# Cross-attention and quantised feed-forward on one core: score maxima copied from one head's block, output normalisation behind head 9, high-part output products first and six of them ahead of the maxima's transposes

## The chip, the core and the metric

The kernel runs on 1 core of one Trainium2 chip. The metric is device time in microseconds (us); smaller is better. Engines are called PE (matrix products), DVE (vector), ACT (activations, copies), POOL (GpSimd) and SP (it issues all DMAs).

## The reference, cut to what matters

There are 16 batches of 256 tokens with 512 features. For every batch:

```python
q = rope(layernorm(x) @ wq.T); k = rope(ctx @ wk.T); v = ctx @ wv.T      # 16 heads of 32
scores = q @ k.T * sqrt(32)          # only |position difference| <= 128 counts
attn = softmax(scores)               # scores are large: the row maximum has to be taken off
x = x + (attn @ v) @ wo.T + wo_b
x = x + ffn(layernorm(x))            # gelu between two matmuls whose inputs are rounded to 16 bit integers
```

The feed-forward part needs the largest absolute value of all normalised rows of all batches before it can begin, and the largest of the hidden layer before its second matmul.

## The kernel before, in words

**Stages.** Stage A (up to some 765 us) does attention batch by batch. Stage B (to some 1,012 us) does the first feed-forward matmul and GELU over 8 tiles of 512 tokens, stage C the second. The change touches stage A alone.

**One step of stage A.** Step b (`step` in each engine's program; `steps` calls it for b = 0 to 15) does three batches at once: the scores, softmax and weighted values of batch b; the projections of batch b+1 (absent in step 15); the output projection of batch b-1 (absent in step 0). So steps 1 to 14 have everything. Every float32 product that needs precision is made of three passes over values split into a high and a low part.

PE's order in a step is written out by hand. First come the 16 heads' scores (`scores`, L597), head pair by head pair, with the projection work of batch b+1 as filling: after pair 0 and 1 the k tiles (and, with pair 1, the transposes of x, L526), after pair 2 the first half of v, after pairs 3 and 4 the q tiles (L514 to L516), after pairs 5 and 6 six products each of the second half of v. The scores go to a ring of two banks, so head n waits until the maximum of head n-2 has been read out (L595). Behind head 15, `o_products` of batch b-1 begins: 24 products (L581), 12 for each half (128 tokens) of the batch, handed out by `some(count)`. Some come before `max_transposes` (L609), four behind it, the rest between the 16 transposed score products (`scores_t`, L631). After heads 7, 11 and 15 of these, and at the end, a `clump` multiplies probabilities with values (L645) and sums the denominators (L658).

DVE's order in a step: masked row maxima of heads 0 to 15 (`row_maxima`, L1063, two passes of 128 rows a head, each followed by a read-out of the maximum), with other work behind the head pairs: behind pair 0 `invert` (L1104, the reciprocal of the denominators of batch b-1, which also frees the bank for PE's x transposes), behind pair 1 `xt_rest`, behind pairs 2 and 3 `rotate` of k (L1086, L1087, L1089), behind pair 5 (head 11) the two `normalise` operations (L1110), which multiply the outputs of batch b-1 by the inverted denominators. Behind head 15 come `split_max` (L1068, L1070: negated maxima in a high and a low part), `rotate` of q, the residual additions, layer norm moments, the quantisation of one weight block and layer norm 1 of batch b+2. 

ACT: after `normalise`, `ot_lead` (L841) rounds the outputs to their high part `t_hi`; after `max_transposes`, two `max_copy` operations (L857) write the maxima as rows 96 to 127 of `q_st` for heads 0 and 1, then for heads 2 and 3; then the 16 exponentials (L864). POOL: `bias_x` (L1374), the low parts of k (`split_lo`, L1358, four operations), the low parts `t_lo` of the outputs (`ot_rest`, L1369), then one band selection a head (L1381).

**The denominators' way.** `invert` writes them to `neg_max`; SP's `spread_shares` stores them to DRAM (L349), waits, and loads them back spread over the rows that need them (L352) into `probs`, called shares here. `normalise` waits for that load. SP issues in program order; in front of these two DMAs stands the load of x_res (L318), which waits until the previous store of it has landed. At the head of step 15, SP first issues two loads of stage B (L357).

**The maxima's way.** `stack_max` (L341 to L344): when both `max_copy` operations are done, SP copies the 32 rows of heads 0 to 3 to heads 4 to 7, 8 to 11 and 12 to 15, three DMAs of 128 KB within SBUF. The transposed scores of heads 4, 8 and 12 wait for one each. All heads have the same rows: each row block of 256 values is repeated for every head.

```python
pe.wait_ge(ot_hi, 2 * j + s + 1)      # L570, in o_products, before its 12 products
pe.wait_ge(ot_lo, 2 * j + s + 1)      # L571
some(4); max_transposes(b, has_proj); some(4)
for n, count in enumerate((1, 2, 2, 3, 1, 1, 1, 0, 1, 1, 1, 0, 1, 1, 0, 0)):
    scores_t(b, n, has_o, has_proj); some(count)
```

Of the kernel before, what the change touches and what calls it, by code (L numbers as in the profile page):

```python
# [22 lines left out]
F32 = mybir.dt.float32  # L23
# [6 lines left out]
P = 128  # L30
NB, S, D = 16, 256, 512
# [3 lines left out]
KC = D // P  # L35
# [3 lines left out]
MROW = 3 * DK  # L39
# [44 lines left out]
def build(nc, t):  # L84
# [12 lines left out]
    with ExitStack() as ctx:  # L97
        def sem(name):
            return ctx.enter_context(nc.semaphore(name))

        def sb(name, shape, dt=F32, where=ctx):
            return where.enter_context(nc.sbuf_tensor(name, shape, dt))
# [16 lines left out]
        w_hi, w_lo = {}, {}  # L119
# [7 lines left out]
        q_st = sb("q_st", [P, H, S], F32R, pa)  # L127
# [5 lines left out]
        t_hi = sb("t_hi", [P, KC, S], F32R, pa)  # L133
        t_lo = sb("t_lo", [P, KC, S], F32R, pa)
# [55 lines left out]
        kv_bank = bank[2:4]  # L190
# [14 lines left out]
        ot_hi, ot_lo = sem("ot_hi"), sem("ot_lo")  # L205
        c_hi, c_lo = sem("c_hi"), sem("c_lo")
        v_mm, o_mm, v_done = sem("v_mm"), sem("o_mm"), sem("v_done")
# [5 lines left out]
        max_stacked = [sem(f"max_stacked{i}") for i in range(1, NC4)]  # L213
        s_mm, max_done, msplit, mT_mm, mT_done = (sem(n) for n in ("s_mm", "max_done", "msplit", "mT_mm", "mT_done"))
# [29 lines left out]
        MAX_COPIES = 2  # L244
# [60 lines left out]
        def _(sp):  # L305
# [32 lines left out]

            def stack_max(b):

                sp.wait_ge(mT_done, MAX_COPIES * (b + 1))  # L341
                for i in range(1, NC4):
                    sp.dma_start(q_st[MROW:P, KC * i:KC * (i + 1)].bitcast(F32),
                                 q_st[MROW:P, 0:KC].bitcast(F32)).then_inc(max_stacked[i - 1], 16)  # L344

            def spread_shares(j):

# [145 lines left out]
            for i in range(NT):  # L493
                for f in range(FC):
                    n, g = (i - KEPT, f + LOADS) if f + LOADS < FC else (i - KEPT + 1, f + LOADS - FC)
# [14 lines left out]
        def _(pe):  # L510
# [7 lines left out]
            def x_transposes(j, s):  # L518

                if s == 0:  # L520
                    pe.wait_ge(ln1_norm, 2 * j + 2)
                    wait(pe, wt_done, j - 1)
                    wait(pe, den_done, j - 1)
                    wait(pe, rope_step["q"], ROPE_OPS * j)
                for c in range(KC):
                    mm = pe.transpose(q_bank[s][:, c * P:(c + 1) * P], x_ln[:, s, c * P:(c + 1) * P], ident[:])  # L526
                mm.then_inc(xt_mm, 1)
# [38 lines left out]
            def o_products(j, has_proj):  # L566

                for s in range(2):
                    tok = slice(s * P, (s + 1) * P)
                    pe.wait_ge(ot_hi, 2 * j + s + 1)  # L570
                    pe.wait_ge(ot_lo, 2 * j + s + 1)  # L571
                    if s == 0:
                        pe.wait_ge(w_lo_done, 5)
                    if has_proj:
                        pe.wait_ge(rope_step["k"], ROPE_OPS * (j + 3))
                    else:
                        pe.wait_ge(res_done, 2 * j)
                    for c in range(KC):
                        parts = ((t_hi, "hi"), (t_hi, "lo"), (t_lo, "hi"))
                        for m, (part, w) in enumerate(parts):  # L580
                            mm = pe.matmul(kv_bank[s][:], part[:, c, tok], (w_hi if w == "hi" else w_lo)["wo"][:, c],  # L581
                                           start=c == 0 and m == 0, stop=c == KC - 1 and m == 2)
                            if c == KC - 1 and m == 2:
                                mm.then_inc(o_mm, 1)
                            yield

            def scores(b, n):

                if n % KC == 0:
                    for name in ("k", "q"):  # L590
                        pe.wait_ge(stacked[name][n // KC], STAGED * (b + 1))
                if n < 2:
                    wait(pe, exp_done, H * b)
                else:
                    pe.wait_ge(max_done, 2 * (H * b + n - 1))  # L595
                for qb in range(2):
                    mm = pe.matmul(ring[n % 2][:, qb * S:(qb + 1) * S], q_st[0:MROW, n, qb * P:(qb + 1) * P],  # L597
                                   k_st[0:MROW, n], start=True, stop=True)
                mm.then_inc(s_mm, 1)

            def max_transposes(b, has_proj):

                pe.wait_ge(msplit, 2 * (b + 1))
                if has_proj:
                    pe.wait_ge(v_done, 2 * (b + 2))
                else:
                    pe.wait_ge(oT_out, 2 * b)
                for qb in range(2):
                    mm = pe.transpose(pv_bank[1][:, qb * P:(qb + 1) * P], neg_max[:, qb], ident[:])  # L609
                mm.then_inc(mT_mm, 1)  # L610
# [89 lines left out]
            def step(b, par, has_c, has_o, has_proj, has_xt):  # L700

                tiles = [[] for _ in range(H // 2)]
                if has_proj:
                    tiles[0] += [lambda: qk_tile(b + 1, "k", 0)]
                    tiles[1] += [lambda: x_transposes(b + 1, 0), lambda: x_transposes(b + 1, 1), lambda: qk_tile(b + 1, "k", 1)]
                    tiles[2] += [lambda: v_tile(b + 1, 0)]
                    tiles[3] += [lambda: qk_tile(b + 1, "q", 0)]
                    tiles[4] += [lambda: qk_tile(b + 1, "q", 1)]
                    tiles[5] += [lambda: v_tile(b + 1, 1, range(2))]
                    tiles[6] += [lambda: v_tile(b + 1, 1, range(2, KC))]  # L710
                for n in range(H):
                    scores(b, n)
                    if n % 2:
                        for tile in tiles[n // 2]:
                            tile()


                heavy = o_products(b - 1, has_proj) if has_o else iter(())

                def some(count):  # L720
                    for _ in range(count):
                        next(heavy, None)

                some(4)
                max_transposes(b, has_proj)
                some(4)
                for n, count in enumerate((1, 2, 2, 3, 1, 1, 1, 0, 1, 1, 1, 0, 1, 1, 0, 0)):
                    scores_t(b, n, has_o, has_proj)
                    some(count)
                    if n in (7, 11, 15):  # L730
                        clump(b, par, n // KC - 1, has_proj)
                assert next(heavy, "none") == "none"
                w_transposes(b, has_proj)
                clump(b, par, NC4 - 1, has_proj)
# [286 lines left out]
        def _(dve):  # L1021
# [77 lines left out]
            def xt_rest(j, s):  # L1099
                rest(q_bank, s, xt_hi, 2 * j + s + 1, xt_lo)  # L1100
# [5 lines left out]
            def normalise(b, half):  # L1106
                dve.wait_ge(oT_out, 2 * b + half + 1)
                dve.wait_ge(share_in, 16 * (b + 1))
                part = oT[:, 2 * half:2 * half + 2].rearrange("p i t -> p (i t)")
                dve.tensor_tensor(part, part, share[:, 2 * half * S:2 * (half + 1) * S], ALU.mult).then_inc(onorm, 1)  # L1110
# [62 lines left out]
            def step(b, par, has_c, has_o, has_proj, has_xt):  # L1173

                between = {p: [] for p in range(H // 2)}
                if has_o:
                    between[0] += [lambda: invert(b - 1)]
                    between[5] += [lambda: normalise(b - 1, 0), lambda: normalise(b - 1, 1)]
                if has_proj:
                    between[1] += [lambda: xt_rest(b + 1, 0), lambda: xt_rest(b + 1, 1)]  # L1180
                    between[2] += [lambda: rotate(b + 1, "k", 0)]
                    between[3] += [lambda: rotate(b + 1, "k", 1)]
                for n in range(H):
                    row_maxima(b, n)
                    if n % 2:
                        for work in between[n // 2]:
                            work()
                split_max(b)
                if has_proj:
                    rotate(b + 1, "q", 0)  # L1190
                    rotate(b + 1, "q", 1)
                if has_o:
                    residual(b - 1, 0)
                    ln2_moments(b - 1, 0)
                quantise_win(b)
                if has_xt:
                    ln1(b + 2)
                if has_o:
                    residual(b - 1, 1)
                    ln2_moments(b - 1, 1)  # L1200
                    largest(b - 1, 0)
                    largest(b - 1, 1)
# [253 lines left out]
```

## Time and profile before

| what | value |
|---|---|
| runs | median 1253.18 us of 3 (1250.85 to 1253.63) |
| the profiled execution, its own time | 1251.07 us |
| its span, first to last instruction | 1249.3 us |
| mean granted PE clock | 0.970 of full |
| PE busy | 1138.1 us, 91% of the span |
| DVE busy | 981.0 us, 79% |
| ACT / POOL busy | 639.6 / 366.4 us |
| one full step of stage A | 43.5 to 44.9 us; granted clock 1.00 from 110 us to 678 us |

Start times are in us from the start of the span. Busy times include overlap of pipelined operations. A matmul's row gives its duration including the pipeline; the distance between two starts says what it costs in a stream. "x4" is a row that merges four instructions; a bracket tells how long the engine was idle before it and who ended the wait.

### The profile page before, as it was taken

The numbers are of one execution on the slowest core, as the hardware profiler recorded it, in microseconds if no ns is written. First come the engines' busy times: TensorE is split into PE (matmuls) and PEld (weight loads), VectorE is DVE, ScalarE is ACT, GpSimd is POOL, SyncE is SP. The second block draws the span as 40 slices with busy tenths as digits, with TensorE's granted clock in tenths as the row PEclk, the third lists the DMA queues.
The fourth block names the chain that finished last, engine by engine and source line by source line (L and its number), as shares of the span: only waits on it lengthen the run. The fifth ranks groups of instructions, "written<-read, shape, count | busy, mean of one in ns | idle before, by whom it ended". The sixth has DMA issues, their size and how long they took to land.

```text
span 1249.3 us, 23318 instructions
## 1 busy us (share of the span) xinstructions
PE 1138.1 (91%) x7776; PEld 759.7 (61%) x7776; DVE 981.0 (79%) x2527; ACT 639.6 (51%) x1000; POOL 366.4 (29%) x540
## 2 busy tenths in 40 slices
PE   5889999999999899999999665999999979999997
PEld 5767777787777688677768443444444434444443
DVE  6769989989988988988899545666666678888885
ACT  5254355335435534543553243555655458777774
POOL 1136336344533634453363220000000030112220
PEclk9889999999999999999999787999999989999999
DMA  8453575566456447545644711455554400567762
GB/s 270 110 143 106 158 178 137 139 183 155 108 161 177 131 134 194 140 120 164 177 119 114 218 56 69 160 206 198 208 188 143 152 0 35 186 224 249 219 207 92
DMA packets 96055, 191.44 MB, mean 153 GB/s; under 512 B 13392, under 2 KB 24912, under 8 KB 95952
## 3 DMA queue, kind: packets, MB, share of 16 engines
q1 hardware_dynamic: 95952, 190.14, 51.5%
q8 instruction: 56, 0.92, 0.3%
q14 instruction: 47, 0.39, 0.1%
HBM read 89.43 MB, written 44.04 MB: 107 GB/s over the span
## 4 chain that ended last, share of the span: by engine, by line
PE 38%; DVE 31%; issue 24%; DMA 3%; SPq 2%; ACT 2%; POOL 0%; DVEq 0%; ACTq 0%; POOLq 0%
PE bank L792 17%; DVE bank L1063 6%; PE bank L514 4%; PE bank L515 4%; PE bank L516 4%; DVE bn L1024 3%; PE bank L597 2%; DVE roped L1089 2%; DVE neg_max L1104 2%; DVE rt L1086 2%; DVE row_max L1063 2%; DVE rt L1087 2%; DVE x_res L1056 1%; PE bank L526 1%; PE bank L581 1%
## 5 line engine op out<-in xcount | busy, mean ns | idle before, releaser
L1063 DVE CUSTOM_DVE_ANT_0 bank<-bank,mask 128x256 f32<-128x256 f32 x512 | 201.4, 454 | 54.6 <-PE bank L597 48.0
L792 PE MATMUL bank<-wout_int,g_hi 128*128 128x512 bf16 x512 | 195.8, 382 | 8.8 <-DVE g_lo L1336 8.7
L792 PE MATMUL bank<-wout_int,g_lo 128*128 128x512 bf16 x512 | 195.6, 382 | 0.0
L761 PE MATMUL bank<-qT_hi,win_int 128*128 128x512 bf16 x512 | 194.2, 379 | 1.4 <-DVE qT_lo L1254 1.4
L761 PE MATMUL bank<-qT_lo,win_int 128*128 128x512 bf16 x512 | 194.1, 379 | 0.0
L864 ACT ACTIVATE probs<-bank 128x512 f32<-128x512 f32 x256 | 142.4, 603 | 52.8 <-PE bank L631 48.3
L1381 POOL TENSOR_SCALAR_AFFINE_SELECT probs<-probs 128x256 f32<-128x256 f32 x256 | 109.1, 430 | 82.9 <-ACT probs L864 78.6
L1336 DVE TENSOR_TENSOR g_lo<-h_int,g_hi 128x512 f16<-128x512 f32 x128 | 104.3, 815 | 35.6 <-ACT g_hi L991 34.3
L597 PE MATMUL bank<-k_st,q_st 96*128 96x256 f32 x512 | 98.4, 306 | 25.7 <-DVE row_max L1063 19.3
L1374 POOL TENSOR_TENSOR x_res<-x_res,wo_b 128x512 f32<-128x512 f32 x32 | 42.0, 1332 | 243.9 <-DMA x_res<-in_x 231.1
L964 ACT ACTIVATE h_ring<-bank,b_in,g_scale 128x512 f32<-128x512 f32 x96 | 73.5, 778 | 75.2 <-PE bank L761 58.1
L1278 DVE TENSOR_REDUCE hmax<-h_ring 128x512 f32 (+1 forms) x96 | 63.4, 682 | 60.6 <-ACT h_ring L964 58.6
L631 PEld LDWEIGHTS bank<-q_st,k_st 128*128 128x128 f32 x512 | 90.3, 193 | 31.8 <-issue 13.6
L597 PEld LDWEIGHTS bank<-k_st,q_st 96*128 96x128 f32 x512 | 76.8, 195 | 50.1 <-DVE row_max L1063 30.8
L631 PE MATMUL bank<-q_st,k_st 128*128 128x256 f32 x512 | 104.1, 294 | 3.1 <-DMA q_st<-q_st 2.0
L991 ACT CAST g_hi<-h_int 128x512 f16<-128x512 f32 x128 | 78.7, 615 | 39.6 <-PE bank L792 31.4
L792 PEld LDWEIGHTS bank<-wout_int,g_hi 128*128 128x128 f16 x512 | 50.4, 98 | 71.4 <-issue 11.2
L1421 POOL TENSOR_TENSOR xq<-xq,b_out 128x512 f32<-128x512 f32 x32 | 48.3, 1540 | 154.5 <-DMA xq<-x_scratch 147.7
L761 PEld LDWEIGHTS bank<-qT_hi,win_int 128*128 128x128 bf16 x512 | 50.1, 98 | 62.3 <-DVE qT_lo L1254 3.1
L792 PEld LDWEIGHTS bank<-wout_int,g_lo 128*128 128x128 f16 x512 | 50.4, 98 | 61.0 <-issue 1.6
L761 PEld LDWEIGHTS bank<-qT_lo,win_int 128*128 128x128 bf16 x512 | 50.1, 98 | 59.2
L514 PE MATMUL bank<-cT_hi,wk_hi 128*128 128x256 f32 x256 | 74.5, 291 | 12.6 <-DVE cT_lo L1141 12.6
(146 smaller groups left out, 2666.2 us busy)
## 6 DMA issues: line engine op xcount, KB each, us to landing
hidden_scratch<-h_ring SPq DMA_DIRECT2D x96, 256.0 KB, 2.0
h_ring<-hidden_scratch SPq DMA_DIRECT2D x96, 256.0 KB, 3.0
k_st<-k_hi SPq DMA_DIRECT2D x128, 128.0 KB, 2.5
q_st<-q_hi SPq DMA_DIRECT2D x128, 128.0 KB, 2.4
xq<-x_scratch SPq DMA_DIRECT2D x16, 1024.0 KB, 6.2
x_ln<-in_x SPq DMA_DIRECT2D x16, 512.0 KB, 4.5
ctx_raw<-in_ctxT SPq DMA_DIRECT2D x16, 512.0 KB, 4.9
k_st<-k_lo SPq DMA_DIRECT2D x64, 128.0 KB, 2.7
```

The costliest lines, as they stand in the source:

```text
L514: pe.matmul(out, l_hi, r_hi, start=first, stop=False)
L597: mm = pe.matmul(ring[n % 2][:, qb * S:(qb + 1) * S], q_st[0:MROW, n, qb * P:(qb + 1) * P], k_st[0:MROW, n], start=True, stop=True)
L631: mm = pe.matmul(third[n][:, kb * S:(kb + 1) * S], k_st[:, n, kb * P:(kb + 1) * P], q_st[:, n], start=True, stop=True)
L761: mm = pe.matmul(bank[f % 4][:], win_int[:, c, f * P:(f + 1) * P], part[:, par, c], start=c == 0 and part is qT_hi, stop=c == KC - 1 and p ...
L792: mm = pe.matmul(bank[4 * par + u][:], part[:, f % 4, u * P:(u + 1) * P], wout_int[:, f], start=f == 0 and part is g_hi, stop=f == FC - 1 ...
L864: act.activation(probs[:, n % SLOTS].rearrange("p k q -> p (k q)"), third[n][:], ACT.Exp, scale=SCORE_SCALE).then_inc(exp_done, 1)
L964: act.activation(dst, bank[f % 4][:], ACT.Gelu, bias=b_in[:, f:f + 1], scale=g_scale[:, f:f + 1]).then_inc(gelu_done, 1)
L991: act.copy(g_hi[:, f % 4], h_int[:, f % 4]).then_inc(ghi_done, 1)
L1063: dve.tensor_tensor_reduce(sc, sc, mask[:, (1 - qb) * P:(1 - qb) * P + S], 1.0, NEG, ALU.add, ALU.max, row_max[:, qb, n:n + 1]).then_inc(m ...
L1278: dve.tensor_reduce(hmax[:, bass.ds(FC * n + f, 1)], src, AX_X, ALU.max, apply_absolute_value=True).then_inc(hmax_done, 1)
L1336: dve.tensor_tensor(g_lo[:, f % 4], h_int[:, f % 4], g_hi[:, f % 4], ALU.subtract).then_inc(glo_done, 1)
L1381: pool.affine_select(out=far, in_=far, compare_op=ALU.is_ge, fill=0.0, base=1 - P, pattern=[[0, 2], [1, P]], channel_multiplier=1).then_in ...
```

## The change

The copy of the maxima now waits for the first `max_copy` only, and takes one head's block (head 0) as its source, repeated over the four heads of each destination. `normalise` goes from behind pair 5 (head 11) to behind pair 4 (head 9). In `o_products` the eight products of `t_hi` of each half come first and the wait for `t_lo` stands behind them, in front of the four products of `t_lo`. Six products instead of four come before `max_transposes`, and one fewer each behind the transposed scores of heads 3 and 13.

```diff
             def stack_max(b):
-                sp.wait_ge(mT_done, MAX_COPIES * (b + 1))
+                sp.wait_ge(mT_done, MAX_COPIES * b + 1)
                 for i in range(1, NC4):
                     sp.dma_start(q_st[MROW:P, KC * i:KC * (i + 1)].bitcast(F32),
-                                 q_st[MROW:P, 0:KC].bitcast(F32)).then_inc(max_stacked[i - 1], 16)
+                                 q_st[MROW:P, 0:1].bitcast(F32).to_broadcast([P - MROW, KC, S])).then_inc(max_stacked[i - 1], 16)
...
                     pe.wait_ge(ot_hi, 2 * j + s + 1)
-                    pe.wait_ge(ot_lo, 2 * j + s + 1)
...
                     for c in range(KC):
-                        parts = ((t_hi, "hi"), (t_hi, "lo"), (t_lo, "hi"))
-                        for m, (part, w) in enumerate(parts):
-                            mm = pe.matmul(kv_bank[s][:], part[:, c, tok], (w_hi if w == "hi" else w_lo)["wo"][:, c],
-                                           start=c == 0 and m == 0, stop=c == KC - 1 and m == 2)
-                            if c == KC - 1 and m == 2:
-                                mm.then_inc(o_mm, 1)
+                        for w in (w_hi, w_lo):
+                            pe.matmul(kv_bank[s][:], t_hi[:, c, tok], w["wo"][:, c], start=c == 0 and w is w_hi, stop=False)
                             yield
+                    pe.wait_ge(ot_lo, 2 * j + s + 1)
+                    for c in range(KC):
+                        mm = pe.matmul(kv_bank[s][:], t_lo[:, c, tok], w_hi["wo"][:, c], start=False, stop=c == KC - 1)
+                        if c == KC - 1:
+                            mm.then_inc(o_mm, 1)
+                        yield
...
-                some(4)
+                some(6)
                 max_transposes(b, has_proj)
                 some(4)
-                for n, count in enumerate((1, 2, 2, 3, 1, 1, 1, 0, 1, 1, 1, 0, 1, 1, 0, 0)):
+                for n, count in enumerate((1, 2, 2, 2, 1, 1, 1, 0, 1, 1, 1, 0, 1, 0, 0, 0)):
...
                 if has_o:
                     between[0] += [lambda: invert(b - 1)]
-                    between[5] += [lambda: normalise(b - 1, 0), lambda: normalise(b - 1, 1)]
+                    between[4] += [lambda: normalise(b - 1, 0), lambda: normalise(b - 1, 1)]
```

## Rows read from the trace of the kernel before

**Rows 1.** Chain of waits, 360 to 420 us: start, duration, engine, tile and line
```profile
373.17 0.68 DVE rt L1086
...
396.22 1.06 PE bank L526 x8
...
410.47 0.31 DVE bank L1063
```

**Rows 2.** Timeline of DVE, step 7, heads 9 to 15: start, duration, instruction, [idle before]
```profile
365.93 0.14 DVE L1063 DVE_READ_ACCUMULATOR2_ANT row_max<- 128x1 f32 x1
366.87 0.43 DVE L1063 CUSTOM_DVE_ANT_0 bank<-bank,mask 128x256 f32<-128x256 f32 x1 [0.80 <-PE bank L597]
...
368.36 1.29 DVE L1110 TENSOR_TENSOR oT<-oT,probs 128x512 f32<-128x512 f32 x2
...
371.94 0.43 DVE L1063 CUSTOM_DVE_ANT_0 bank<-bank,mask 128x256 f32<-128x256 f32 x1
```

**Rows 3.** Timeline of POOL, step 7, same stretch
```profile
365.37 2.83 POOL L1358 TENSOR_TENSOR k_lo<-roped,k_hi 128x256 fp32r<-128x256 f32 x4 [1.75 <-ACT k_hi L810]
```

**Rows 4.** Timeline of DVE, then of POOL, step 2
```profile
149.11 1.19 DVE L1110 TENSOR_TENSOR oT<-oT,probs 128x512 f32<-128x512 f32 x1
...
146.94 2.81 POOL L1358 TENSOR_TENSOR k_lo<-roped,k_hi 128x256 fp32r<-128x256 f32 x4 [1.71 <-ACT k_hi L810]
```

**Rows 5.** Timeline of DVE, then of POOL, stage C
```profile
1020.47 1.54 DVE L1336 TENSOR_TENSOR g_lo<-h_int,g_hi 128x512 f16<-128x512 f32 x1
1021.93 1.49 DVE L1315 TENSOR_SCALAR h_int<-h_int,wout_man 128x512 f32<-128x512 f32 x1
...
1021.43 1.70 POOL L1421 TENSOR_TENSOR xq<-xq,b_out 128x512 f32<-128x512 f32 x1
```

**Rows 6.** Timeline of PE, step 7, heads 13 to 15
```profile
370.06 0.40 PE L516 MATMUL bank<-wv_hi,cT_lo 128*128 128x512 f32 x1
370.49 0.50 PE L597 MATMUL bank<-k_st,q_st 96*128 96x256 f32 x2
...
373.31 0.44 PE L609 MATMUL bank<-ident,neg_max 128*128 128x128 f32 x2 [0.39 <-DVE neg_max L1070]
```

**Rows 7.** Timeline of DVE, first pass of head 10, steps 1 and 14
```profile
104.01 0.43 DVE L1063 CUSTOM_DVE_ANT_0 bank<-bank,mask 128x256 f32<-128x256 f32 x1 [0.65 <-PE bank L597]
...
673.88 0.43 DVE L1063 CUSTOM_DVE_ANT_0 bank<-bank,mask 128x256 f32<-128x256 f32 x1 [0.34 <-PE bank L597]
```

**Rows 8.** Line L352 (shares) summed up; its issue in step 11; DVE, head 9 there
```profile
DMA to landing us min/median/max: 3.5/3.7/5.3
...
537.08 0.58 SPq L352 DMA_DIRECT2D probs<-den_scratch  x1
...
541.76 0.14 DVE L1063 DVE_READ_ACCUMULATOR2_ANT row_max<- 128x1 f32 x1
```

**Rows 9.** Landing of L343 (maxima), of L349 (denominators); PE, head 4, step 8
```profile
DMA to landing us min/median/max: 2.2/2.3/4.0
...
DMA to landing us min/median/max: 1.7/3.9/7.2
...
422.59 0.50 PE L631 MATMUL bank<-q_st,k_st 128*128 128x256 f32 x2 [1.30 <-DMA q_st<-q_st]
```

**Rows 10.** Timelines of ACT (head 4), of DVE and of PE behind `split_max`, step 7
```profile
377.77 0.60 ACT L864 ACTIVATE probs<-bank 128x512 f32<-128x512 f32 x1 [0.34 <-PE bank L631]
...
386.19 0.68 DVE L286 SCALAR_TENSOR_TENSOR nt_t<-nt_t,veps 128x2 f32<-128x2 f32 x1
...
392.73 0.42 DVE L1063 CUSTOM_DVE_ANT_0 bank<-bank,mask 128x256 f32<-128x256 f32 x1
...
391.71 0.74 PE L597 MATMUL bank<-k_st,q_st 96*128 96x256 f32 x4
```

**Rows 11.** Timeline of DVE, then of PE, step 15 and the end of stage A
```profile
719.84 1.29 DVE L1110 TENSOR_TENSOR oT<-oT,probs 128x512 f32<-128x512 f32 x2 [7.71 <-DMA probs<-den_scratch]
...
753.42 0.76 PE L581 MATMUL bank<-wo_hi,t_hi 128*128 128x512 f32 x1 [10.29 <-ACT t_hi L841]
```

## The prediction, made before the changed kernel was run

> **What bounds the kernel now.** I read the chain of waits first, then the timelines of DVE, PE and POOL around the lines that the change moves. The busy shares (PE 91%, DVE 79%) are averages over three stages. In stage A the chain of waits changes engines three times in a step [rows 1]: from `split_max` (373.1) it lies on DVE without a gap, through rotation, moments, weight block and layer norm, up to `invert`; at 396.22 it goes to PE, whose x transposes need the bank that `invert` frees; at 410.47 it comes back to DVE at head 10 and stays there, through `normalise` and heads 12 to 15, until PE's transposes of the maxima. So DVE is the bound behind `split_max` and again behind head 10; PE is it between. The x transposes start 23.2 us behind `split_max` (373.06 in this step) in 11 of steps 1 to 13, 23.5 in step 6 and 24.4 in step 8.
>
> **Normalisation behind head 9.** First what it gives. In step 7 the last maximum of head 9 is read out from 365.93 and DVE idles until head 10's scores come, at 366.87 [rows 2]: 0.94 us, into which a part of `normalise` now fits. `normalise` costs 1.21 us (368.36 to the head 12 start at 369.57).
>
> Then what it meets. POOL's four low-part operations of k run from 365.37 to 368.20 [rows 3], 0.70 us each: head 9 ends 0.55 us into them, in every step. `normalise` now comes behind them. The trace shows what a DVE operation with two operands in SBUF does beside such an operation of POOL. In step 2 the first `normalise` took 1.19 us where 0.68 is the median: POOL ended 0.64 behind its start, and it ended 0.55 later [rows 4]. In stage C they take turns: DVE's operation from 1020.47 ends 0.58 behind POOL's (1021.43), POOL's next takes 1.70 where the one before took 1.26, and DVE's next, begun at 1021.93, ends behind that one [rows 5]. The Trainium skill says the same more sharply (SBUF — State Buffer, Who interferes with whom): a DVE instruction with two SBUF inputs and a GpSimd instruction that reads SBUF lock one another out for a whole instruction. By that rule moving `normalise` here is the wrong way round, and the trace agrees.
>
> The block worked out from head 9's read-out: 0.15 until POOL's current operation ends, 0.57 for the first `normalise`, 0.57 for POOL's next (0.73, less the overlap of their ends), 0.55 for the second, less 0.08 until the next maximum can begin: 1.76 us. Bounds: 1.21 if they don't meet, 2.5 if the second waits for two. I take 1.76: the rows are of the same kinds of instruction, and one of them is `normalise` beside this very operation.
>
> Step 7 then: head 10 begins at 365.93 + 1.76 = 367.69, not 366.87; head 11 0.73 later, 368.42; its maximum is out and seen by PE 0.96 later, 369.38. Head 13's scores wait for that (ring of two banks). Behind them come 0.33 and six v products at 0.235, so head 14's scores start at 371.12 instead of 370.49 [rows 6] (370.06 + 0.235 is where PE would have been by itself), DVE takes head 14 0.59 behind that and head 15 0.73 later: 372.44 instead of 371.94 [rows 2]. All of step 7 costs +0.50. In general, with i the time between head 9's read-out and head 10, and B the length of the present block, the cost is 1.44 - i - (B - 1.21). I read i and B in all 14 steps (head 10 of the first and last: [rows 7]): in seven i is 0.72 to 0.95 and B 1.21, cost 0.49 to 0.72, together 3.9; in the other seven i is 0.13 to 0.59 and B up to 1.72, cost 0.79 to 0.81, together 5.6. **Sum +9.5.**
>
> **Shares.** `normalise` waits for L352, which lands 3.5 to 5.3 us behind its issue [rows 8]. At head 9 it has landed in 11 steps. In three it has not: step 3 by 0.32, step 8 by 0.23, step 11 by 0.62 (537.08 + 5.3 against 541.76 [rows 8]); each then meets one more POOL operation, 0.70. **+2.1.** Behind the waiting `normalise` stand the maxima 10 and 11, and behind these PE's heads 12 and 13. SP, ACT and POOL queues keep their order; `t_lo` comes earlier, and PE needs it three products or more later: no cost.
>
> **Copy of the maxima.** SP issues it 0.53 us earlier, one `max_copy`. Head 4 now comes one product (0.235) earlier, so it needs the DMA to land within 2.45 + 0.53 - 0.24 = 2.74 us; it lands in 2.3 at the median [rows 9]. Its source rows are now runs of 1 KB instead of 4 KB. The nearest row with 1 KB runs and 128 KB is L349: 1.7, 3.9 and 7.2, but that goes to DRAM and mostly behind another DMA. I take 2.3 and keep 1.7 and 3.9. The Trainium skill (DMA: Bandwidth & Descriptors, Why small descriptors are slow) puts the penalty of small pieces on HBM alone; by it the landing stays and the sum too. In step 8 the copy landed late and PE waited 1.30 [rows 9]: 0.3 less of it.
>
> **Six products ahead.** Between head 15's scores and the transposes PE idles 0.39 behind four products [rows 6], and by my step 7 it would idle 0.7 behind six: two products (0.47) go into a hole, no cost. Head 4's transposed scores come one product earlier; ACT idled 0.34 there for PE [rows 10], so exponentials, POOL's band selections and low parts move up by 0.235. PE's own gain is worth nothing at first, since DVE is the bound there: it takes head 0 1.02 behind PE's start (392.73 against 391.71 [rows 10]) where 0.69 would do. But DVE's layer norm chain is paced by POOL: an operation on two values a row takes 0.68 beside it [rows 10]. I take 0.2 of the 0.235 for the 13 steps (1 to 13) that run on into `invert`; bounds 0 and 0.33. With step 8: **-2.9.** The product taken from behind head 13 gains nothing: the last clump waits for ACT and POOL. High part first: the same 24 products, no cost.
>
> **Step 15 and the end.** The shares are late there by 7.71 us [rows 11]. Heads 10 and 11 were done in that wait; now they stand behind it, two of 0.75, and PE's heads 12 and 13 behind them (products stand 0.43 apart there, not 0.235, after PE's long wait). Worked through as above, `split_max` comes 1.96 later than now; six products at that distance end at about the same time: **+1.9** (1.5 to 2.8). At the end the output products start with `t_hi` done (752.65) instead of behind `t_lo` (753.42 [rows 11]): **-0.7.**
>
> **Sum:** 9.5 + 2.1 - 2.9 + 1.9 - 0.7 = +9.9 us on the profiled execution's own 1251.07, so 1261. That execution lies 2.1 below the median of the runs; 9.9 on the median is 1263. I say 1262.
>
> **Rivals.** (a) *The two engines don't meet*, or POOL yields: the block is 1.21. Then 0.55 less in 14 steps and some 1.3 less for the late shares: +0.9, 1252 to 1255. For it: in seven present steps they don't meet; against: the overlap at the new place is there in all 14. (b) *Faster:* the maxima 10 and 11 don't hold PE, since PE's filling covers them; head 14 and 15 come as PE can bring them, head 15 at 371.62 instead of 371.94, 0.32 in 14 steps, and with -2.9, +1.9 and -0.7 it is -6.2: 1245 to 1247. It decides at head 10: its start must not be over 0.3 us later than now. For it: the hole of 0.94; against: seven steps have under 0.6. (c) *The new copy lands at 3.9.* PE's head 4 then comes 0.9 later than now, 0.33 of it hidden at head 0: 0.6 in 14 steps and no gain: +21, 1272. (d) *The move gives no earlier normalisation*, the shares being late in most steps: 0.7 in 11 more steps, 1269. Against it: they land 0.4 to 3.1 us early in 11 steps.
>
> **Chances:** forecast 0.52, (a) 0.15, (b) 0.17, (c) 0.11, (d) 0.05. The forecast's own range is 1256 to 1267, from 1.6 to 1.9 us of block and 0 to 0.33 of gain. The whole range, 1250.5 to 1272, takes in (a), (d) and (c). Within 0.2% (2.5 us, about what a measurement of this kernel can tell from no change) is most of (a): 0.15; faster is (b), 0.17; slower the rest, 0.68.
>
> **What the changed profile would show.** Right: L1110 pairs of 1.8 us and more beside L1358, where each operation took 0.70; DVE idle no longer before head 10 but before head 14; a wait of PE for row_max before heads 12 and 13; steps of 44.2 to 44.8 us; L343 at 2.3. Wrong: L1110 pairs of 1.3 us; the chain not on DVE behind head 10; the x transposes not some 23.0 behind `split_max`; L631 waiting for L343 in many steps.

## The result, and the profile of the changed kernel

The changed kernel takes 1264.58 us (median of 4 runs, 1263.05 to 1265.07), the kernel before 1253.10 (4 runs, 1250.85 to 1253.63). The ratio is 1.0093, with a 95% interval of 1.0076 to 1.0110: slower. The profiled execution took 1265.07 us, with a span of 1263.3 and a mean granted clock of 0.967.

Lines behind L570 have moved, most of them by one: scores L598, maxima L1064, `normalise` L1111, low parts of k L1359, `t_lo` L1370, `bias_x` L1375, products of `t_hi` L579 and of `t_lo` L583.

The page's busy times, DMA packets and the group of the scores:

```profile
PE 1136.5 (90%) x7732; PEld 762.4 (60%) x7776; DVE 984.9 (78%) x2527; ACT 641.0 (51%) x1000; POOL 378.3 (30%) x540
...
DMA packets 100663, 191.44 MB, mean 152 GB/s; under 512 B 13392, under 2 KB 31056, under 8 KB 100560
...
L598 PE MATMUL bank<-k_st,q_st 96*128 96x256 f32 x512 | 96.2, 304 | 38.3 <-DVE row_max L1064 32.0
```

The group of the scores in the kernel before:

```profile
L597 PE MATMUL bank<-k_st,q_st 96*128 96x256 f32 x512 | 98.4, 306 | 25.7 <-DVE row_max L1063 19.3
```

PE is busy 1.6 us less than before, and the kernel is 11.5 slower: no work was added, the engines wait more. DVE's and POOL's busy times rose by 3.9 and 11.9 us for the same work: their operations hold each other up, as the next rows show. In front of the scores PE waits 32.0 us for the maxima (19.3 before).

Step 7 in DVE's timeline, from `normalise` on, answers to [rows 2]; the fourth line is head 14, the fifth head 15:

```profile
372.19 0.14 DVE L1064 DVE_READ_ACCUMULATOR2_ANT row_max<- 128x1 f32 x1
372.19 1.88 DVE L1111 TENSOR_TENSOR oT<-oT,probs 128x512 f32<-128x512 f32 x2
374.00 0.42 DVE L1064 CUSTOM_DVE_ANT_0 bank<-bank,mask 128x256 f32<-128x256 f32 x1
...
378.01 0.43 DVE L1064 CUSTOM_DVE_ANT_0 bank<-bank,mask 128x256 f32<-128x256 f32 x1 [0.71 <-PE bank L598]
...
378.74 0.47 DVE L1064 CUSTOM_DVE_ANT_0 bank<-bank,mask 128x256 f32<-128x256 f32 x1
...
379.90 0.19 DVE L1071 SCALAR_TENSOR_TENSOR neg_max<-row_max,neg_max 128x32 fp32r<-128x32 f32 x1
```

POOL in the same stretch [rows 3]:

```profile
371.64 3.71 POOL L1359 TENSOR_TENSOR k_lo<-roped,k_hi 128x256 fp32r<-128x256 f32 x4 [1.71 <-ACT k_hi L811]
375.32 2.52 POOL L1370 TENSOR_TENSOR t_lo<-oT,t_hi 128x512 fp32r<-128x512 f32 x2
```

And PE [rows 6]: heads 12, 13, then 14 and 15, and the transposes of the maxima:

```profile
375.00 0.47 PE L598 MATMUL bank<-k_st,q_st 96*128 96x256 f32 x2 [0.71 <-DVE row_max L1064]
375.67 0.50 PE L598 MATMUL bank<-k_st,q_st 96*128 96x256 f32 x2 [0.20 <-DVE row_max L1064]
...
377.42 0.65 PE L598 MATMUL bank<-k_st,q_st 96*128 96x256 f32 x4
...
380.15 0.44 PE L610 MATMUL bank<-ident,neg_max 128*128 128x128 f32 x2 [0.67 <-DVE neg_max L1071]
```

What the prediction drew is there. From `normalise` to head 10's first pass it is 1.81 us (372.19 to 374.00). POOL's four operations took 3.71 where they took 2.83. DVE's idle time went from before head 10 to before head 14. Head 15 starts 6.55 us behind head 9's last read-out (378.74 - 372.19); before it was 6.01 (371.94 - 365.93).

**The steps.** I cut each step of both traces at two places: from one `split_max` to the first x transpose (X), and from there to the next `split_max` (Y). Of the 14.0 us between the spans, 0.58 come before the first `split_max`, 11.50 in steps 1 to 14 (615.03 became 626.53), 1.77 in step 15 and 0.15 behind it.

| sums over 14 steps, us | before | after | difference | forecast |
|---|---|---|---|---|
| X, `split_max` to x transposes | 327.22 | 322.65 | -4.57 | -2.9 |
| Y, x transposes to `split_max` | 287.81 | 303.88 | +16.07 | +11.6 |

X is 23.15 before and 22.92 after in most steps. In four of the steps the shares come late (3, 5, 11 and 13: `normalise` waits 0.17, 0.74, 0.81 and 0.51). Three of these cost 2.29, 2.05 and 2.97 in Y; the other eleven steps 8.8 together.

Step 11, DVE, then PE at head 12:

```profile
550.96 2.29 DVE L1111 TENSOR_TENSOR oT<-oT,probs 128x512 f32<-128x512 f32 x2 [0.81 <-DMA probs<-den_scratch]
...
554.18 0.47 PE L598 MATMUL bank<-k_st,q_st 96*128 96x256 f32 x2 [2.07 <-DVE row_max L1064]
```

The same place in windows (PEclk is the mean over the window, and a window can hold both clock levels):

```profile
core 0: us, PE busy (x) PEld busy (x) DVE busy (x) ACT busy (x) POOL busy (x), PEclk, DMA share, GB/s
551.00:555.00 4.00, 1.73 (x8) 1.01 (x7) 3.95 (x11) 1.14 (x2) 2.72 (x3) 1.00 0.01 3
555.00:558.00 3.00, 3.00 (x13) 2.60 (x14) 1.64 (x9) 0.58 (x1) 1.50 (x2) 0.68 0.00 0
558.00:562.00 4.00, 4.00 (x19) 3.10 (x18) 3.86 (x14) 1.45 (x3) 0.00 (x0) 0.81 0.00 0
```

`normalise` waited 0.81 us for the shares and then took 2.21 us until head 10, which came 1.36 later than in a step with its shares in time: two of POOL's operations of 0.70. PE stood still for 2.07 us, and after that the granted clock was 0.68 and 0.81 on the mean of 7 us (1.00 there before): for a part of them products came 0.43 apart instead of 0.235, the lower of the two levels.

Step 15, DVE and PE [rows 11], and the way of the maxima [rows 9]:

```profile
731.71 1.29 DVE L1111 TENSOR_TENSOR oT<-oT,probs 128x512 f32<-128x512 f32 x2 [9.96 <-DMA probs<-den_scratch]
...
738.69 0.19 DVE L1071 SCALAR_TENSOR_TENSOR neg_max<-row_max,neg_max 128x32 fp32r<-128x32 f32 x1
...
739.74 0.63 PE L610 MATMUL bank<-ident,neg_max 128*128 128x128 f32 x2
...
L343 SPq DMA_DIRECT2D q_st<-q_st x48: 601/607/678, 67.1 to 742.3; - x48
...
DMA to landing us min/median/max: 2.3/2.4/4.3
```

From `normalise` to `split_max` it is 6.98 us there (5.00 before). The transposes come 1.05 behind `split_max` (0.25 before), because six products at 0.43 us outlast it. The new counts do that, not the move: in experiment 1 it is 0.25 with the move alone and 1.04 with all but the move. The new copy lands in 2.4 us at the median, with four times as many packets: the page's count rose by 4608, 96 for each of 48 copies.

### The profile page after: what moved, and what is told of

The parts are those of the page before. It is cut to its first block, busy times and chain, and to the rows that moved or that the text cites. A ratio compares the mean times of both kernels' runs of the same rounds, so it can differ in the third digit from the quotient of the medians.

```text
span 1263.3 us, 23258 instructions
## 1 busy us (share of the span) xinstructions
PE 1136.5 (90%) x7732; PEld 762.4 (60%) x7776; DVE 984.9 (78%) x2527; ACT 641.0 (51%) x1000; POOL 378.3 (30%) x540
## 4 chain that ended last, share of the span: by engine, by line
PE 33%; DVE 30%; issue 25%; DMA 5%; SPq 4%; ACT 2%; DVEq 0%; POOL 0%; ACTq 0%; POOLq 0%
PE bank L793 16%; DVE bank L1064 6%; SPq L336 3%; PE bank L514 3%; PE bank L515 3%; PE bank L516 3%; DVE bn L1025 2%; DVE roped L1090 2%; DVE rt L1087 2%; PE bank L598 2%; DVE rt L1088 2%; DMA den_scratch<-neg_max 2%; DVE row_max L1064 2%; DMA probs<-den_scratch 2%; PE bank L632 1%
## 5 line engine op out<-in xcount | busy, mean ns | idle before, releaser
L1064 DVE CUSTOM_DVE_ANT_0 bank<-bank,mask 128x256 f32<-128x256 f32 x512 | 201.6, 456 | 59.2 <-PE bank L598 51.6
L793 PE MATMUL bank<-wout_int,g_hi 128*128 128x512 bf16 x491 | 187.5, 382 | 8.8 <-DVE g_lo L1337 8.6
L762 PE MATMUL bank<-qT_hi,win_int 128*128 128x512 bf16 x489 | 185.4, 379 | 0.0
L598 PE MATMUL bank<-k_st,q_st 96*128 96x256 f32 x512 | 96.2, 304 | 38.3 <-DVE row_max L1064 32.0
L1375 POOL TENSOR_TENSOR x_res<-x_res,wo_b 128x512 f32<-128x512 f32 x32 | 42.0, 1333 | 244.3 <-DMA x_res<-in_x 231.7
L598 PEld LDWEIGHTS bank<-k_st,q_st 96*128 96x128 f32 x512 | 76.6, 197 | 61.1 <-issue 45.5
```

Of the source, the lines that this page charges most:

```text
L762: mm = pe.matmul(bank[f % 4][:], win_int[:, c, f * P:(f + 1) * P], part[:, par, c], start=c == 0 and part is qT_hi, stop=c == KC - 1 and p ...
L793: mm = pe.matmul(bank[4 * par + u][:], part[:, f % 4, u * P:(u + 1) * P], wout_int[:, f], start=f == 0 and part is g_hi, stop=f == FC - 1 ...
L1064: dve.tensor_tensor_reduce(sc, sc, mask[:, (1 - qb) * P:(1 - qb) * P + S], 1.0, NEG, ALU.add, ALU.max, row_max[:, qb, n:n + 1]).then_inc(m ...
```

## The experiments

All ratios are to the kernel before on the same chip, with 95% intervals. "X", "Y" and "block" (from `normalise` to head 10 or 12) are read as above.

**1. The move of `normalise` alone, and all but that.** First edit on the kernel before, second on the changed kernel:

```diff
-                    between[5] += [lambda: normalise(b - 1, 0), lambda: normalise(b - 1, 1)]
+                    between[4] += [lambda: normalise(b - 1, 0), lambda: normalise(b - 1, 1)]
```
```diff
-                    between[4] += [lambda: normalise(b - 1, 0), lambda: normalise(b - 1, 1)]
+                    between[5] += [lambda: normalise(b - 1, 0), lambda: normalise(b - 1, 1)]
```

> The kernel before with the normalisation alone moved behind head 9. Theory (the move is the whole loss: two engines taking turns, late shares, maxima 10 and 11 behind them, step 15): all terms of the loss without the two gains, 9.5 + 2.1 + 1.9 = 13.5 over 1253, so 1264 to 1269; pairs of L1110 take 1.8 us and over. Rival (the loss is in the copy of 1 KB runs or in the products' new order): this kernel stays within 3 us of 1253.

> The changed kernel with the normalisation back behind head 11. Theory: the gains are left, 2.9 to 4.7 in the steps and 0.7 at the end, so 1248 to 1250, and the x transposes stay 22.9 behind split_max. Rival (copy or order costs): 1256 or more.

Measured: the move alone 1269.65 us, 1.0129 [1.0114, 1.0144]; all but the move 1249.08 us, 0.9968 [0.9957, 0.9980]. The move costs 15.5 us (1264.58 - 1249.08) beside the other edits and 16.5 without them. The other edits gain 4.0. The changed kernel is a small gain and a large loss. The loss itself was a little above what I had worked out (1269.65 against 1264 to 1269).

The trace of the move alone says what late shares are worth. There they were late in one of the 14 steps (step 8), with pairs of 1.79 to 1.81 us in all of them. From head 9's last read-out to `split_max` the 14 steps took 11.1 us more than before; in the changed kernel, with four late steps, 16.0 more. That is 4.9 us for three more late steps, the clock behind two of them included.

**2. Is it the two engines' turn-taking?** In the changed kernel POOL's two `t_lo` operations go ahead of the four of k, so that POOL waits for `normalise` instead of running beside it:

```diff
-                if has_proj:
-                    for c in range(KC):
-                        split_lo("k", b + 1, c)
                 if has_o:
...
                     ot_rest(b - 1, 1)
+                if has_proj:
+                    for c in range(KC):
+                        split_lo("k", b + 1, c)
```

> The changed kernel, but POOL does the low parts of the outputs before the low parts of k, so that no POOL work stands beside the normalisation behind head 9. Theory (turn-taking costs 0.59 of the 1.80 us block, in 14 steps, and a POOL operation each where shares are late): 8 us less than the changed kernel, 1255 to 1258, pairs of L1110 at 1.2 to 1.3. It could give some back if q's rotation then waits for k's low parts. Rival (only the late shares and the longer way over PE cost, not the turns): within 2 us of 1264.6.

Measured: 1258.47 us, 1.0038 [1.0024, 1.0052]. In step 7, DVE and POOL:

```profile
369.14 1.29 DVE L1111 TENSOR_TENSOR oT<-oT,probs 128x512 f32<-128x512 f32 x2
370.35 0.43 DVE L1064 CUSTOM_DVE_ANT_0 bank<-bank,mask 128x256 f32<-128x256 f32 x1
...
376.54 0.19 DVE L1071 SCALAR_TENSOR_TENSOR neg_max<-row_max,neg_max 128x32 fp32r<-128x32 f32 x1
...
371.16 2.53 POOL L1370 TENSOR_TENSOR t_lo<-oT,t_hi 128x512 fp32r<-128x512 f32 x2 [4.52 <-ACT t_hi L842]
373.65 2.82 POOL L1359 TENSOR_TENSOR k_lo<-roped,k_hi 128x256 fp32r<-128x256 f32 x4
```

`normalise` has its 1.21 us back, POOL's four operations take 2.82 again, and the block is 1.20 to 1.22 in every step. So the turn-taking is real, and without it the kernel is 6.1 us faster (1264.58 - 1258.47). That is not its price alone. Head 10 comes 0.60 earlier in a step, but from head 10 to `split_max` it now takes 6.18 us and took 5.90 in the changed kernel, so 0.32 a step is left, 4.5 in 14 steps; the rest lies in the late shares, which are other steps in another execution.

It isn't the whole loss either. In the kernel before, head 10 to `split_max` took 6.20 us with `normalise` in it (366.87 to 373.06 in step 7), and here it takes 6.18 without (370.35 to 376.54): the 1.21 us that left the place behind head 11 give nothing back in such a step, since PE's scores set the pace there (DVE idles 0.73 before head 14). In front, the pair of 1.21 fills a hole of 0.94 or less. Without any turns and late shares the move costs 5.9 us in the 14 steps of this trace.

The shares are still late in steps 3, 4, 5 and 15, and by 0.15 us in 8 and 13. And POOL's `bias_x`, which starts when the load of x_res lands, meets another DVE operation with two inputs, the rotation of k. Steps 8 and 9 of this kernel, DVE and then POOL:

```profile
410.31 1.48 DVE L1090 TENSOR_TENSOR roped<-rt 128x512 f32<-128x512 f32 x1
...
454.95 0.87 DVE L1090 TENSOR_TENSOR roped<-rt 128x512 f32<-128x512 f32 x1
...
409.95 3.00 POOL L1375 TENSOR_TENSOR x_res<-x_res,wo_b 128x512 f32<-128x512 f32 x2 [16.92 <-DMA x_res<-in_x]
...
452.73 2.54 POOL L1375 TENSOR_TENSOR x_res<-x_res,wo_b 128x512 f32<-128x512 f32 x2 [15.07 <-DMA x_res<-in_x]
```

In step 8 `bias_x` began 0.36 us ahead of the rotation's last operation, which took 1.48 us; in step 9 it had begun 2.2 us ahead and was nearly through, and the operation took 0.87. Heads 8 and 9 came 0.6 later by it. The step's Y was 21.73, the next one's 20.83; the other 0.3 is from the shares, late by 0.15 in step 8.

**3. Step 15 alone.** The changed kernel, with `normalise` behind head 11 in the last step:

```diff
-                    between[4] += [lambda: normalise(b - 1, 0), lambda: normalise(b - 1, 1)]
+                    between[4 if has_proj else 5] += [lambda: normalise(b - 1, 0), lambda: normalise(b - 1, 1)]
```

> The changed kernel with the normalisation behind head 9 in steps 1 to 14, behind head 11 in step 15. Theory: heads 10 and 11 go back into the wait for the shares there: 1.9 less (1.5 to 2.8), 1261.8 to 1263.1. Rival (step 15's loss was not this): no difference.

Measured: 1262.99 us, 1.0069 [1.0053, 1.0085], 1.6 less than the changed kernel, but the two intervals overlap, so the medians alone don't show it. The traces do: from `normalise` to `split_max` in step 15 it is 5.00 to 5.01 us in each of the eight traces with `normalise` behind head 11, and 6.98 to 6.99 in each of the four with it behind head 9. The two kernels are the same program up to step 15, yet here the shares were late in steps 2, 3, 5, 8, 10 and 13, and in the changed kernel in 3, 5, 11 and 13; the sums of Y agree (303.06 and 303.88). Which step is hit differs between executions of the same code. That the sums agree is chance: with the move alone (experiment 1) one step was hit, and the 14 steps cost less.

**4. Where the gain comes from.** Three edits on the kernel before: the product counts alone, the copy alone, and both (without the high part first).

```diff
-                some(4)
+                some(6)
...
-                for n, count in enumerate((1, 2, 2, 3, 1, 1, 1, 0, 1, 1, 1, 0, 1, 1, 0, 0)):
+                for n, count in enumerate((1, 2, 2, 2, 1, 1, 1, 0, 1, 1, 1, 0, 1, 0, 0, 0)):
```
```diff
-                sp.wait_ge(mT_done, MAX_COPIES * (b + 1))
+                sp.wait_ge(mT_done, MAX_COPIES * b + 1)
...
-                                 q_st[MROW:P, 0:KC].bitcast(F32)).then_inc(max_stacked[i - 1], 16)
+                                 q_st[MROW:P, 0:1].bitcast(F32).to_broadcast([P - MROW, KC, S])).then_inc(max_stacked[i - 1], 16)
```

> The kernel before with the counts alone changed: six products ahead of the maxima's transposes, one fewer each behind heads 3 and 13 (old copy, high and low parts mixed, normalisation behind head 11). Theory: the product taken from before head 4's transposed scores is the gain; x transposes come 22.9 instead of 23.2 behind split_max, 3 us in all: 1250 (1249 to 1251). It might lose a little where the old copy, issued later, now comes too late for head 4 (2.3 against 2.2 allowed), which would show as waits of L631 for the copy. Rival (the earlier copy brings the 0.24): nothing here, 1253.

> The kernel before with the new copy of the maxima alone. Theory: it lands 2.4 behind an issue that is 0.5 earlier, nobody waits for it, so nothing: 1253, or up to 1.5 less where a copy of before came late (step 8). Rival (runs of 1 KB cost): later landing, 1255 or more.

> The kernel before with the new copy and the new counts, high and low parts mixed as before, normalisation behind head 11. Theory (only together do they let head 4's transposed scores come earlier: with the counts alone PE waited for the copy, with the copy alone PE was not there): x transposes 22.9 behind split_max, where each alone had 23.15, and 1249.5 to 1250.5. Rival (the high part first brings the gain): 1252.5 as each alone.

Measured: counts alone 1252.70 us, 0.9992 [0.9978, 1.0005]; copy alone 1252.54, 0.9989 [0.9977, 1.0001]; both 1249.05, 0.9957 [0.9943, 0.9971]. The counts alone, from which I had expected the whole gain (1250), came out as the rival said. X is 23.15 with either alone and 22.91 with both. The views of waits, of counts alone and then of copy alone, say why:

```profile
PEld bank L631 <- DMA q_st<-q_st: 7.0, 15, 1.2
```
```profile
PEld bank L631 <- DMA q_st<-q_st: 0.7, 1, 0.7
```

With one product fewer ahead of it, head 4 finds the old copy not yet there, in 15 steps, some 0.4 us each (its weight load waited 0.14 before, so the slack was already gone); with the copy issued earlier and the old counts there is slack, which nobody uses. Together they move PE 0.24 forward. All but the move of `normalise`, which has the high part first too, is as fast as both together (1249.08 and 1249.05): the order of the high part gave nothing that the medians can show.

**5. Earlier shares.** SP issues the denominators' two DMAs ahead of the load of x_res, first with the changed kernel, then with `normalise` behind head 7 as well:

```diff
                 if has_o:
-                    load_xres(b - 1)
                     spread_shares(b - 1)
+                    load_xres(b - 1)
```

> The changed kernel, but SP moves the denominators and shares before it waits for the store of x_res. Shares then land some 3 us earlier and no normalisation of steps 1 to 14 waits for them. Theory (late shares, each with a POOL operation more and at times a lower clock behind it, are 3 to 6 us of the loss; turn-taking stays): 1257 to 1261, pairs of L1110 at 1.8 in all 14 steps; step 15's wait some 2 us shorter. Rival (turn-taking is all): less than 2 us off 1264.6.

> The changed kernel with the shares moved first as in the run above, and the normalisation behind head 7 and k's rotation, so before POOL's low parts of k begin. Theory: the pair takes 1.2 to 1.3, DVE reaches head 10 at most 0.4 late, and behind head 11 nothing stands between the maxima, so head 15 comes up to 0.3 earlier than before the change: 1243 to 1249. Rival (DVE lateness at heads 8 and 9 holds PE): 1250 or more, with waits of PE for row_max at heads 10 and 11.

Measured: 1266.38 us, 1.0096 [1.0074, 1.0118], and 1291.29 us, 1.0300 [1.0280, 1.0321]. Both are misses, by 5 and by over 40 us. The shares did come in time in steps 1 to 14, in both. But the load of x_res moved back with them, and `bias_x` behind it, to where `normalise` is. The profiled execution of the second took 1279.92 us, the fastest of its six and 11.4 below their median, so its trace shows only a part of that loss. Step 4 of the first, DVE and then POOL:

```profile
237.41 2.96 DVE L1111 TENSOR_TENSOR oT<-oT,probs 128x512 f32<-128x512 f32 x2
...
236.13 2.54 POOL L1375 TENSOR_TENSOR x_res<-x_res,wo_b 128x512 f32<-128x512 f32 x2 [18.40 <-DMA x_res<-in_x]
```

A DVE operation now waits for POOL operations of 1.27 us instead of 0.70: the block was 2.31 to 2.89 in seven steps of the first kernel and 2.31 to 3.27 in eleven of the second. The second shows both sides in two neighbouring steps:

```profile
378.02 2.82 DVE L1111 TENSOR_TENSOR oT<-oT,probs 128x512 f32<-128x512 f32 x2
...
424.58 1.29 DVE L1111 TENSOR_TENSOR oT<-oT,probs 128x512 f32<-128x512 f32 x2
...
376.14 3.00 POOL L1376 TENSOR_TENSOR x_res<-x_res,wo_b 128x512 f32<-128x512 f32 x2 [16.78 <-DMA x_res<-in_x]
...
426.25 2.53 POOL L1376 TENSOR_TENSOR x_res<-x_res,wo_b 128x512 f32<-128x512 f32 x2 [19.69 <-DMA x_res<-in_x]
```

Beside `bias_x` the pair took 2.82 us, ahead of it 1.29. The rival of this run showed as well. In step 7, PE waited 1.71 us for head 8's maximum in front of head 10, and the clock fell behind it:

```profile
381.68 0.51 PE L598 MATMUL bank<-k_st,q_st 96*128 96x256 f32 x2 [1.71 <-DVE row_max L1064]
...
383.56 0.63 PE L516 MATMUL bank<-wv_hi,cT_lo 128*128 128x512 f32 x1
383.99 0.63 PE L514 MATMUL bank<-wv_hi,cT_hi 128*128 128x512 f32 x1
```

In six steps of this trace head 10 to `split_max` took 7.7 us, where it took 6.2 to 6.3 in seven others. I had looked at what the shares waited for, not at what the load of x_res releases. So this pair doesn't price the late shares: it took one cost away and brought another.

**6. POOL's new order with `normalise` behind head 11.** If experiment 2 gives 6 us by order alone, does it help where `normalise` was?

> The changed kernel with the normalisation behind head 11 and POOL's low parts of the outputs before those of k. Theory: nothing of POOL stands beside the normalisation, all pairs take 1.21 where some of before took 1.3 to 1.7, but there DVE was late already, so it gains 0.1 to 0.3 in a few steps only: 1247 to 1249.5, if k's low parts, some 3 us later, hold neither q's rotation nor the stacking DMAs. Rival: they do, and it takes 1252 or more.

Measured: 1278.42 us, 1.0205 [1.0188, 1.0223]. The block is 1.21 in every step, and the kernel is 29 us slower than with POOL's old order. POOL in step 8, and the line of waits for 400 to 445 us:

```profile
428.66 2.52 POOL L1370 TENSOR_TENSOR t_lo<-oT,t_hi 128x512 fp32r<-128x512 f32 x2 [4.85 <-ACT t_hi L842]
431.14 2.77 POOL L1359 TENSOR_TENSOR k_lo<-roped,k_hi 128x256 fp32r<-128x256 f32 x4
...
DVE rt L1087 <- POOL k_lo L1359: 1.4, 1, 1.4
```

DVE's rotation of q, behind `split_max`, waits for the low parts of k, and these now end at 433.9. DVE stands still for 1.4 us on its critical stretch, and the two operations of `split_max` took 1.47 us beside those of POOL, where they took 0.4 before; X is 24.6 to 26.0 from step 2 on in place of 22.9.

**7. What makes the shares of step 15 late.** Two loads of 1 MB for stage B stand in front of them in SP's order. In the kernel with all but the move of `normalise` they go behind:

```diff
                     spread_shares(b - 1)
+                if not has_proj:
+                    load_xq(0, 0)
+                    load_xq(1, 1)
...
                     sp.wait_ge(qk_mm["k"], 2 * NB)
-                    load_xq(0, 0)
-                    load_xq(1, 1)
```

> The changed kernel with the normalisation behind head 11, and the two loads of stage B that SP issues at the head of step 15 put behind the denominators and shares of that step. Theory (the 7 to 10 us of waiting for shares in step 15 is mostly the denominators' store of 7.2 us behind these two loads): the store lands in 2 to 4, the shares 3.5 to 5 us earlier, and the kernel takes 1244 to 1246 where all_but_n9 took 1249.1. Rival (PE and DVE of step 15 are bound elsewhere, or stage B then waits for the late loads): no difference.

Measured: 1244.75 us (1243.07 to 1246.33), 0.9931 [0.9917, 0.9944]. It is the fastest of all kernels here, 8.9 us below the kernel before on that chip and 4.3 below the kernel that it is made from. SP and DVE in step 15:

```profile
704.36 0.47 SPq L349 DMA_DIRECT2D den_scratch<-neg_max  x1
708.36 0.58 SPq L352 DMA_DIRECT2D probs<-den_scratch  x1
708.98 1.15 SPq L357 DMA_DIRECT2D xq<-x_scratch  x2
...
712.40 1.29 DVE L1112 TENSOR_TENSOR oT<-oT,probs 128x512 f32<-128x512 f32 x2 [3.67 <-DMA probs<-den_scratch]
```

The store of the denominators landed within 4.0 us of its issue, `normalise` waited 3.67 us, and step 15 took 40.18 us. In the kernel that it is made from, with the two loads in front, it was 8.4, 8.47 and 45.12 (before [rows 9, rows 11]: 7.2, 7.71 and 44.60). Step 15 took 43.4 to 47.0 us in all seven traces with the loads in front and `normalise` behind head 11, so 40.18 is well outside that scatter.

## Why the prediction was right

The forecast was 1262 with its own range 1256 to 1267; 1264.58 lies in it, and the mechanism is the one described. That the number came so near is in part luck: two terms were too small, one on each side. Term by term:

- **The block** (forecast 1.76 us): 1.79 to 1.83 in the steps with shares in time. In step 7 head 15 comes 0.54 later than before, counted from head 9 (forecast 0.50); heads 14 and 15 are set by PE, and PE idles 0.67 ahead of the transposes (forecast 0.7). In the ten steps with the shares in time it costs 7.5 from head 9's read-out to `split_max`; the formula that gave 9.5 for 14 gives 6.9 for these ten. This term held, and experiment 2 shows that the turns are part of it: without them about 0.3 a step is left of the 0.6 in step 7. Of the rows from which I took the turns, one of stage C (L1315 [rows 5]) is no operation with two tensors in SBUF; those of step 2 and the first DVE row of stage C carry the argument.
- **Late shares** (+2.1): too small. Steps 3 and 11 were named rightly, step 8 was not late and 5 and 13 were. I had priced each late step at one POOL operation, 0.70, the wait included. That is what steps 3 and 13 show: head 10 came 0.69 and 0.68 later than with shares in time. In steps 5 and 11 it came 1.39 and 1.36 later, two operations: `normalise` could start only 0.88 and 0.95 us behind head 9's read-out, when the next of them had begun too (0.15 + 0.70). In steps 3 and 11 the granted clock fell besides, and that was in no term: head 10 to `split_max` took 6.67 and 6.56 instead of 5.90. Together the four steps took 5.8 more than the formula for their block, where the term had 2.1.
- **The gain** (-2.9): -4.57. The 0.2 a step was 0.24. Another 1.25 is the late copy of step 8 before [rows 9], which didn't recur, so the step behind it lost no time; I had taken 0.3 of it. That part is luck and no gain of the change: the new copy came late as well, with waits of PE of 0.9 to 1.4 us in one to three steps of six other traces. My reason was half of the truth: I gave the gain to the counts, on the condition that the copy lands within 2.74 us of an earlier issue. The runs show that condition to be all of the copy's part: neither edit has a gain alone.
- **Step 15** (+1.9): 1.98 more from `normalise` to `split_max`. The transposes came 0.8 later still, because the six products outlast `split_max` by 1.05; I had that as "at about the same time". In the medians the place costs 1.6, within their scatter.
- **The end** (-0.7): the first output product starts 2.00 behind the last `normalise` (2.78 before), as said, but the last one ends only 0.3 earlier relative to it (9.91 against 10.18). Over all traces it is 9.5 to 10.3 in the eight with the high part first and 10.2 to 10.9 in the five without, 0.6 on the mean, so the term is about right; this pair shows less of it, and the medians can't show it. The products begin at the low clock level and rise to the high one on the way: before, the first eight stood 0.43 apart and the rest 0.235, now ten or eleven of them stand 0.43 apart. In this pair slower products took back most of what the earlier start gave.
- The forecasts that fell short or long cancel in part: the steps took 11.5 where the terms gave 8.7, the start of the program 0.6 more. Against the medians the difference is 11.5, against the profiled executions 14.0; the one of before lay 2 us below its median and the one of after at the top of its runs.

Of the rivals, (a) is excluded by the block of 1.8, (b) by the steps' length, (c) by the landing of 2.4 us, (d) by 10 of 14 steps without a wait for shares. The rule that the prediction quoted from the Trainium skill (SBUF — State Buffer, Who interferes with whom) holds here: a two-input DVE operation and one of POOL shut each other out for whole instructions, 1.81 us against 1.21. The run that takes it away is 6.1 us faster, the largest part of the loss that a run has priced.

**What stays open.** The 16.0 us that steps 1 to 14 of the changed kernel's trace lost from head 9's read-out to `split_max` can be split, with the trace of experiment 2, into 5.9 for the hole that is too small while PE sets the pace behind it, 4.5 for the turns, and the remaining 5.6 for late shares with the clock behind them; step 15 adds 2.0. This is a reading of single executions, in which the late steps fall by chance, and the parts add up to more than the 15.5 us of the medians. Against the medians only the 6.1 us of experiment 2 is a measured difference. `bias_x` beside the rotation of k also costs, but not more than before: head 9 comes 13.25 to 14.26 us behind the x transposes, and the sums over 14 steps are 0.07 apart in the two traces. No run separates the late shares: experiment 5 was to do it and moved `bias_x`. A kernel with early shares and `bias_x` kept where it is wasn't tried.

## What to carry to other kernels

Before a DVE operation with two SBUF operands is moved into a hole, read POOL's timeline at the new place: the hole of 0.94 us was real, but beside POOL the pair of 1.21 became 1.81. Read also what sets the pace at the old place: behind head 11 it was PE, and DVE's freed time bought nothing there. When a DMA is moved on a queue, follow also the one that it passes, up to the work that its landing releases. And a DMA that is late for no visible reason is worth a look at what stands ahead of it in its queue's order: the largest single gain here (4.3 us, beside 4.0 for the copy and the counts together) was two large loads that had no hurry.

## What the runs showed of the hardware that I had not expected

- A copy within SBUF of 128 KB cut into 128 packets lands as fast (2.4 us) as one in 32 (2.3).
- A DVE pair of two-input operations takes 1.21 us alone, 1.8 beside POOL operations of 0.70, and 2.3 to 3.3 beside those of 1.27. POOL's four operations grow from 2.83 to 3.71 too.
- A hole in PE's work can cost clock, but its length alone doesn't tell. PE idled 1.39 us in step 3, 1.85 in step 5 and 2.07 in step 11 of the changed kernel. Behind the first the granted clock was 0.71 on the mean of 196 to 200 us and behind the third 0.68 on that of 555 to 558; behind the second it stayed at 1.00.
